# Feed-forward's tail in two halves, the projection's statistics one tile later, and the first experts' rows asked for a block ahead with their stores on ScalarE

## The chip, the cores and the metric

The kernel is one program on one core of a Trainium2 chip. The metric is device time in microseconds (us), the median of the runs. TensorE has two clock levels, 1.2 and 2.4 GHz; the profile gives the granted clock as a share of the higher one.

## The reference

A graph network over 3125 rows of 256 numbers and 53125 edges, four residual stages in a row:

```
x = x + gnn0(layernorm(x))     # attention over edges, projection, LN1, feed-forward, LN2
x = x + moe0(layernorm(x))     # 8 experts, top 2, hidden 256
x = x + gnn1(layernorm(x))     # two graph convolutions
x = x + moe1(layernorm(x))     # 8 experts, top 2, hidden 1024
```

The change lies in the end of gnn0 and in moe0:

```
h1  = layer_norm(h + attn_out, ln1_g, ln1_b)          # h is layernorm(x); attn_out = out @ Wp + bp
ffn = gelu(h1 @ W1 + b1) @ W2 + b2                    # 256 -> 1024 -> 256
x   = x + layer_norm(h1 + ffn, ln2_g, ln2_b)
t   = layernorm(x);  p = softmax(t @ router_w.T)
out = t + sum over the top 2 experts e of  w_e * (gelu(t @ w1[e] + b1[e]) @ w2[e] + b2[e])
x   = x + out
```

All of it is in float32.

## The kernel before

Rows are kept in SBUF in 25 tiles of 128 (`NT`), X (the residual), R (work) and ST (the statistics of `bn_stats`, six numbers a tile and partition). Each stage is a `Block` in which every engine has its own instruction list; a stage begins when all engines have left the one before. Within it, engines are ordered by semaphores alone (`wait_ge`, `then_inc`), and each engine takes its instructions strictly in order. SyncE (SP) issues nearly all plain DMAs, GpSimd (POOL) the indirect ones. `Chain` makes every step of VectorE (DVE) wait for the one before it.

**Projection, `attention_out` (L1094).** For each tile VectorE divides the sums by the weights (L1131, two tiles ahead), TensorE turns the tile and multiplies it by Wp (L1169, L1178), ScalarE (ACT) copies the turned tile in between (L1159), and VectorE adds h (L1140), adds the bias and writes R (L1144), then takes R's statistics (L1147). L1144 waits for L1140 and L1147 for L1144. `over_tiles` runs the first two tiles straight, then eleven loop rounds of two, then the last.

**Feed-forward, `ffn_blocks` (L1186).** 13 blocks of two tiles (`BR` = 2, the last holds one real tile). VectorE's step j: `prepare(j+1)` (normalise two tiles L612, times gamma L1240, plus beta L1243), copy of the turned block (L1249), then when TensorE has y(j): add the rows (L1257), add b2 and write R (L1260), statistics of R (L1264). TensorE's step j: eight hidden products (L1302), the turn of block j+1 (L1292), which needs `prepare(j+1)`, then y (L1311). ScalarE does the eight gelus (L1279). Before and after it `finish_ln` (L199) turns ST into RSTD and NMR with seven small steps of VectorE and a Sqrt of ScalarE.

**The tail, `ffn` (L1388).** In five chunks of 6, 6, 5, 5 and 3 tiles: ScalarE normalises R (L1419), VectorE multiplies by gamma (L1440), GpSimd adds beta to X (L1431), VectorE adds R to X (L1442) and takes X's statistics (L1445). `Logits` (L1320) follows tile by tile once a chunk's X is there: TensorE turns it (L1355), ScalarE copies it (L1381), TensorE multiplies it by the router (L1362). Before the first turn stands a product of ones with the router's weights (L1368). The router's weights are SyncE's second DMA of the block (L1342), after gamma and beta (L1408).

**First experts, `experts(k, 0)` (L1695).** GpSimd scatters the normalised rows to slots in HBM that are sorted by expert (L1826), and raises `landed` after each group of four tiles. Blocks of 256 slots are run in an order computed on the chip, 29 of them here (j = 0 to 28), each with a table word that gives its slot and its expert (`block_of`, a table load on the engine that asks). For block j:

- SyncE, `step`: `load_rows(j)` (waits for the turn of block j-2 and for `landed`; L1767), waits for y(j-2) by `y_done`, `store(j-2)` (waits for `y_ready`; L1778), `load_rest(j)` (L1772). All in this order, in one queue.
- ScalarE: waits for y(j-1), copies the weights of block j+1 from `every` to `pack` (L1915), then two gelus (L1926).
- TensorE: hidden product (L1958), turn of block j+1 (L1943, needs its rows), y (L1967). The turn writes the one buffer `pT`, which VectorE copies (L1860).
- VectorE: copy of the turned block (L1860), y plus b2 (L1870), which must find its y buffer stored.

GpSimd gathers the results back per group of tiles once the stores it needs have landed (L1846), and after the last block VectorE sums each tile's two results with the residual (L1877, L1883) and takes statistics (L1888). In the second experts layer (`layer` = 1) the same functions run with larger weights.

Of the kernel before, what the change touches and what calls it, by code (L numbers as in the profile page):

```python
# [189 lines left out]
def at(i, n=1):  # L190
    return bass.ds(i, n)
# [902 lines left out]
def attention_out(k):  # L1094
# [3 lines left out]
    with ExitStack() as s:  # L1098
# [87 lines left out]
def ffn_blocks(k):  # L1186
# [5 lines left out]
    nc, a, C, R, ST = k["nc"], k["a"], k["C"], k["R"], k["ST"]  # L1192
# [8 lines left out]
    BLOCKS = -(-NT // BR)  # L1201
    with ExitStack() as s:
# [19 lines left out]
        y_ready, fin, norm, scaled = sem("_y_ready"), sem("_finish"), sem("_norm"), sem("_scaled")  # L1222
        block = s.enter_context(nc.Block())

        @block.sync
        def _(sp):
            sp.dma_start(gb[:], a["rows0"][:, 1:3, :]).then_inc(gb_in, 16)
            sp.dma_start(pack[:], a["ffn"][0]).then_inc(pack_in, 16)

        @block.vector  # L1230
        def _(dve):
# [19 lines left out]
            def step(j, b, i, first, last):  # L1251
# [11 lines left out]
                for r in range(BR):  # L1263
                    dve.bn_stats(ST[:, at(BR * j + r), :], R[:, at(BR * j + r), :])  # L1264

            dve.wait_ge(gb_in, 16)
# [3 lines left out]
            over_tiles(dve, step, BLOCKS)  # L1270

        @block.scalar
        def _(act):
# [9 lines left out]
            over_tiles(act, step, BLOCKS)  # L1283
# [104 lines left out]
def ffn(k):  # L1388

    nc, a, X, R, ST = k["nc"], k["a"], k["X"], k["R"], k["ST"]  # L1390
    finish_ln(k, "1")
    ffn_blocks(k)
    finish_ln(k, "2")
    with ExitStack() as s:
        gb = s.enter_context(nc.sbuf_tensor("ln2_rows", [P, 2, D], F32))
        gb_in, normed = s.enter_context(nc.semaphore("ln2_rows_in")), s.enter_context(nc.semaphore("normed"))
        step_done, x_ready = s.enter_context(nc.semaphore("ffn_step")), s.enter_context(nc.semaphore("ffn_x_ready"))
        b_added = s.enter_context(nc.semaphore("ln2_b_added"))
        chunks_ = [(c, slice(lo, hi)) for c, (lo, hi) in enumerate(((0, 6), (6, 12), (12, 17), (17, 22), (22, NT)))]
# [3 lines left out]
        def wide(part):  # L1403
            return [P, part.stop - part.start, D]

        @block.sync
        def _(sp):
            sp.dma_start(gb[:], a["rows0"][:, 3:5, :]).then_inc(gb_in, 16)  # L1408
# [7 lines left out]
        def _(act):  # L1416
            for c, part in chunks_:
# [9 lines left out]
        @block.gpsimd  # L1427
        def _(pool):
            pool.wait_ge(gb_in, 16)
            for c, part in chunks_:  # L1430
                pool.tensor_tensor(X[:, part, :], X[:, part, :], gb[:, 1:2, :].to_broadcast(wide(part)),  # L1431
                                   ALU.add).then_inc(b_added, 1)

        @block.vector
        def _(dve):
            link = Chain(dve, step_done)
            dve.wait_ge(gb_in, 16)
            for c, part in chunks_:
                dve.wait_ge(normed, c + 1)
                link(dve.tensor_tensor(R[:, part, :], R[:, part, :], gb[:, 0:1, :].to_broadcast(wide(part)), ALU.mult))  # L1440
                dve.wait_ge(b_added, c + 1)
# [253 lines left out]
def experts(k, layer):  # L1695
# [17 lines left out]
    with ExitStack() as s:  # L1713
# [45 lines left out]
        def _(sp):  # L1759
# [19 lines left out]

            def step(j, b, i, first, last):  # L1780
# [19 lines left out]
            n = over_blocks(sp, step)  # L1800
            e = load_rows(2 * n + 1, 1, 2 * n)
            store(2 * n - 1, 1, 2 * n)
            load_rest(e, 1)
            store(2 * n, 0, 2 * n + 1)
            for landed_, count in [(y_out[0], n + 1), (y_out[1], n), (rows_in[0], n + 1), (rows_in[1], n + 1),
                                   (rest_in[0], n + 1), (rest_in[1], n + 1)]:
# [105 lines left out]
        def _(act):  # L1912
# [4 lines left out]
            def step(j, b, i, first, last):  # L1917
# [16 lines left out]
            over_blocks(act, step)  # L1934
# [578 lines left out]
```

## Time and profile before

| | |
|---|---|
| median of three runs | 2792.26 us (2792.14 to 2793.42) |
| the profiled execution | 2789.74 us, span 2787.7 us |
| TensorE (PE) busy | 2289.8 us, 82% of the span |
| VectorE (DVE) busy | 1490.0 us, 53% |
| ScalarE (ACT) busy | 1246.7 us, 45% |
| GpSimd (POOL) busy | 716.6 us, 26% |
| granted clock, mean | 0.927 |
| projection, start of the first division to the last statistics | 1053.3 to 1107.2 us |
| feed-forward's blocks, first hidden product to last statistics | 1120.0 to 1309.5 us |
| tail of the feed-forward, first DMA to copied logits | 1312.5 to 1361.7 us |
| first experts, first turn to the turn after the last block | 1409.1 to 1547.7 us |

The busy shares are means over stages with different limits and say little about any one of them. Times in the rows are microseconds from the start of the span. `PEld` is TensorE's weight load, which runs beside its products; `SPq` is an instruction of SyncE's queue. A pair in square brackets is the time that the engine was idle before the instruction and what released it.

### The profile page before, as it was taken

The page shows a single profiled execution, that of the slowest core. Times are in us where ns is not written, and L with a number is a line of the kernel's source. Part 1 is how long each engine was busy: PE and PEld are TensorE (multiplying, and loading weights), DVE is VectorE, ACT ScalarE, POOL GpSimd, SP SyncE. Part 2 cuts the span into 40 slices and gives each one's busy share as a digit, 9 for nine tenths or more (in the row PEclk, how much of TensorE's full clock was granted, in tenths as well). Part 3 has the DMA queues.
Part 4 walks back from the last instruction along what each step waited for, and adds up shares of the span by engine and source line. Part 5 has one row for each costly group of instructions (what it writes and reads, how often), then busy time and mean ns, then how long its engine had stood idle before and what let it go on. Part 6 is the DMA issues. An engine that isn't in the chain of part 4 may idle for free. (4 is left out here: it accounts for less than half of the span.)

```text
span 2787.7 us, 50123 instructions
## 1 busy us (share of the span) xinstructions
PE 2289.8 (82%) x10903; PEld 1803.5 (65%) x10904; DVE 1490.0 (53%) x2999; ACT 1246.7 (45%) x2511; POOL 716.6 (26%) x720
## 2 busy tenths in 40 slices
PE   1688876889989895997468399995999954999995
PEld 0344443666666663886456288884888853888884
DVE  7799975898888887332733644544002153111113
ACT  1799943777777772223223122343324431222221
POOL 0000011777777770000374311000110006002013
PEclk9999997999999998999589699997999956999998
DMA  5421222777777770000166322221222105656555
GB/s 196 200 76 73 76 82 81 208 212 213 212 212 212 213 203 20 22 0 4 49 212 193 109 76 70 69 67 53 67 67 74 55 2 189 218 191 221 189 204 178
DMA packets 183896, 353.28 MB, mean 127 GB/s; under 512 B 55346, under 2 KB 138727, under 8 KB 179111
## 3 DMA queue, kind: packets, MB, share of 16 engines
q1 hardware_dynamic: 138328, 206.94, 22.9%
q0 software_dynamic: 45520, 145.80, 18.1%
q8 instruction: 18, 0.29, 0.0%
q14 instruction: 30, 0.25, 0.0%
HBM read 275.32 MB, written 77.31 MB: 126 GB/s over the span
## 5 line engine op out<-in xcount | busy, mean ns | idle before, releaser
L2279 PE MATMUL gnn_p<-gnn_y,gnn_counts_wide 128*128 (+1 forms) x2500 | 553.6, 381 | 2.7 <-DVE R_kept L2161 2.6
L2279 PEld LDWEIGHTS gnn_p<-gnn_y,gnn_counts_wide 128*128 128x128 f32 x2500 | 473.1, 191 | 69.1 <-DVE R_kept L2161 6.6
L856 POOL DMA_INDIRECT kv_pair<-kv,gather_idx x448 | 428.1, 956 | 150.6 <-issue 103.6
L2084 ACT CAST gnn_counts_wide<-gnn_counts 128x1664 f32<-128x1664 uint16 x100 | 158.0, 1580 | 387.1 <-PE gnn_p L2279 368.0
L956 PE MATMUL p_edge_q<-QX_kept,onehot_turned 128*128 x904 | 264.1, 415 | 61.6 <-ACT onehot_turned L919 54.7
L1926 ACT ACTIVATE experts_hidden<-experts_p_hidden,experts_pack 128x256 f32<-128x256 f32 x290 | 134.1, 472 | 337.3 <-PE experts_p_hidden L1958 337.3
L1958 PE MATMUL experts_p_hidden<-experts_turned,experts_pack 128*128 128x256 f32 x1160 | 263.6, 383 | 2.1 <-DVE experts_turned L1857 1.2
L956 PEld LDWEIGHTS p_edge_q<-QX_kept,onehot_turned 128*128 128x128 f32 x904 | 155.4, 191 | 166.6 <-issue 151.1
L1967 PE MATMUL experts_p_y<-experts_pack,experts_hidden 128*128 128x256 f32 x1160 | 260.2, 379 | 0.0
L1958 PEld LDWEIGHTS experts_p_hidden<-experts_turned,experts_pack 128*128 128x128 f32 x1160 | 222.7, 192 | 33.6 <-issue 2.8
L964 PE MATMUL p_sums<-R_kept 128*128 128x264 f32 x896 | 237.3, 388 | 0.0
L564 PE MATMUL adj_p<-adj_onehot_src,adj_onehot_key 128*128 128x416 f16 x1200 | 231.4, 343 | 6.3 <-DVE adj_onehot_src L538 4.6
L1967 PEld LDWEIGHTS experts_p_y<-experts_pack,experts_hidden 128*128 128x128 f32 x1160 | 215.9, 190 | 27.3 <-ACT experts_hidden L1926 0.2
L1846 POOL DMA_INDIRECT experts_back<-slots_out,CSLOT x100 | 97.5, 975 | 417.0 <-issue 416.4
L908 ACT ACTIVATE dst_distance<-WHERE_kept,DST_kept 128x128 f32 x456 | 158.3, 394 | 67.2 <-issue 67.1
L538 DVE TENSOR_SCALAR adj_onehot_src<-adj_count_src,adj_src_in_quarter 128x832 f16<-128x832 f16 x500 | 181.3, 430 | 0.0
L1857 DVE TENSOR_SCALAR experts_turned<-experts_p_turned,experts_rest 128x256 f32<-128x256 f32 x60 | 29.8, 539 | 278.6 <-DMA experts_rest<-experts 252.4
L564 PEld LDWEIGHTS adj_p<-adj_onehot_src,adj_onehot_key 128*128 128x128 f16 x1200 | 110.0, 98 | 94.4 <-DVE adj_onehot_src L538 5.3
L883 DVE TENSOR_TENSOR qk_prod<-kv_pair,p_edge_q 128x528 f32<-128x528 f32 x224 | 156.2, 697 | 20.4 <-DMA kv_pair<-kv,gather_idx 14.1
L964 PEld LDWEIGHTS p_sums<-R_kept 128*128 128x128 f32 x896 | 153.4, 191 | 15.0 <-DVE ACC_kept L875 0.3
L888 DVE TENSOR_REDUCE qk_sum<-qk_prod 128x16 f32<-128x528 f32 x224 | 155.6, 694 | 0.0
L2253 POOL TENSOR_TENSOR R_kept<-gnn_y,gnn_brows 128x256 f32 x50 | 39.2, 784 | 451.8 <-DVE gnn_y L2137 438.1
(376 smaller groups left out, 3214.2 us busy)
## 6 DMA issues: line engine op xcount, KB each, us to landing
experts_pack<-experts SPq DMA_DIRECT2D x29, 2052.0 KB, 8.8
gnn_counts<-adj SPq DMA_DIRECT2D x400, 104.0 KB, 2.2
adj<-adj_counts SPq DMA_DIRECT2D x100, 208.0 KB, 1.9
experts_rows<-slots_in SPq DMA_DIRECT2D x60, 256.0 KB, 3.8
slots_out<-experts_y SPq DMA_DIRECT2D x58, 256.0 KB, 7.7
experts_rest<-experts SPq DMA_DIRECT2D x60, 130.0 KB, 8.0
kv_pair<-kv,gather_idx POOLq DMA_INDIRECT x448, 3.8
slots_in<-R_kept SPq DMA_DIRECT2D x2, 3328.0 KB, 13.9
```

What stands on the lines that cost most here:

```text
L538: ins = dve.tensor_scalar(ohs[p][:, c, :], count[:], column(smod, t + c), None, ALU.is_equal)
L564: mm = pe.matmul(pA[p][:, c, 0:QS // 2], ohk[p][:, n, :], ohs[p][:, n, c * (QS // 2):(c + 1) * (QS // 2)], start=False, stop=False)
L856: pool.indirect_dma_start(kv[r][:, j, :], None, a["kv"], bass.IndirectOffsetOnAxis(ap=idx[r][:, j:j + 1], axis=0)).then_inc(kv_in[r], 16)
L883: dve.tensor_tensor(prod[:], kv[r][:, :, 0:QW], pQ[q][:, :, 0:QW], ALU.mult).then_inc(prod_ready, 1)
L888: dve.tensor_reduce(red[q][:].rearrange("p j h -> p (j h)"), prod[:].rearrange("p j (h c) -> p (j h) c", c=HD + 1), AX.X, ALU.add).then_in ...
L908: ins = act.activation(dist[q][:, j, :], where[:, at(w), :].squeeze(1), ACT.Square, scale=-1.0, bias=column(k["DST"], t + j))
L956: mm = pe.matmul(pQ[q][:, j, 0:QW], oht[q][:, j, :], QX[:, at(w), :].squeeze(1), start=True, stop=True)
L964: mm = pe.matmul(pA[q][:, 0:VW], oh[r][:, j, :], wv[r % 4][:, j, :], start=(j == 0), stop=(j == GT - 1))
L1958: mm = pe.matmul(pH[c][:, 0:BT], w[:, lo:lo + P], tT[b][:, d, :], start=(d == 0), stop=(d == KD - 1))
L1967: mm = pe.matmul(pY[b][r][:, 0:D], hid[b][:, h, r * P:(r + 1) * P], w[:, W2 + h * D:W2 + (h + 1) * D], start=(h == 0), stop=(h == HC - 1))
L2084: act.copy(wide[b][:], raw[r][:].rearrange("p q s -> p (q s)")).then_inc(wide_ready, 1)
L2279: mm = pe.matmul(bank[:, off:off + D], wide[b][:, j * P:(j + 1) * P], y[:, at(n), :].squeeze(1), start=first and off == 0, stop=last and ( ...
```

## The change

Four edits.

1. *Projection.* `bn_stats` of tile n-1 is placed between L1140 and L1144 of tile n; that of the last tile follows the loop.
2. *Feed-forward.* Gamma and beta of the second LN are loaded at the start of `ffn_blocks`, and GpSimd adds beta to all of X there. After step 5 (of 0 to 12) VectorE works out the variance of tiles 0 to 11, ScalarE takes its root after its step 6, and VectorE finishes the factors after its own step 6. After each of the steps 7 to 12 VectorE finishes two of these tiles (`add_early`): normalise, times gamma, add to X, statistics of X.
3. *Tail.* Only tiles 12 to 24 are left to finish, in chunks of 5, 4 and 4. Tiles 0 to 11 need no wait before their turn. After normalising each chunk ScalarE copies four turned tiles of the first twelve, then the rest.
4. *First experts.* SyncE's `light_step(j)` asks for the rows of block j+1, waits for y(j-2) by `y_ready`, and asks for the rest of block j. The stores are issued by ScalarE: `store(j-1)` after the gelus of block j. The rows asked for past the last block stay, the rest asked for past it does not. The second experts layer keeps its order.

```diff
@@ attention_out, VectorE's step
+                if not first or b:
+                    spread_of(n - 1)
                 dve.wait_ge(part_ready, n + 1)
                 dve.scalar_tensor_tensor(out=R[:, at(n), :], ...).then_inc(r_ready, 1)
+
+            def spread_of(n):
                 dve.wait_ge(r_ready, n + 1)
                 dve.bn_stats(ST[:, at(n), :], R[:, at(n), :])
...
             over_tiles(dve, step)
+            spread_of(NT - 1)
@@ ffn_blocks
+    HALF = (BLOCKS - 1) // 2
+    EARLY = BR * HALF
...
             sp.dma_start(pack[:], a["ffn"][0]).then_inc(pack_in, 16)
+            sp.dma_start(ln2[:], a["rows0"][:, 3:5, :]).then_inc(ln2_in, 16)
+
+        @block.gpsimd
+        def _(pool):
+            pool.wait_ge(ln2_in, 16)
+            for lo in range(0, NT, 5):
+                pool.tensor_tensor(X[:, lo:lo + 5, :], X[:, lo:lo + 5, :], ln2[:, 1:2, :].to_broadcast([P, 5, D]),
+                                   ALU.add).then_inc(ln2_added, 1)
...
+            def add_early(p):
+                tiles = at(BR * p, BR)
+                for r in range(BR):
+                    tile = R[:, at(BR * p + r), :]
+                    normalise(dve, k, tile, tile, BR * p + r).then_inc(early_normed, 1)
+                dve.wait_ge(early_normed, BR * p + BR)
+                dve.tensor_tensor(R[:, tiles, :], R[:, tiles, :], ln2[:, 0:1, :].to_broadcast([P, BR, D]),
+                                  ALU.mult).then_inc(early_scaled, 1)
+                dve.wait_ge(early_scaled, p + 1)
+                dve.tensor_tensor(X[:, tiles, :], X[:, tiles, :], R[:, tiles, :], ALU.add).then_inc(early_x, 1)
+                dve.wait_ge(early_x, p + 1)
+                for r in range(BR):
+                    dve.bn_stats(ST[:, at(BR * p + r), :], X[:, at(BR * p + r), :])
...
-            over_tiles(dve, step, BLOCKS)
...
+            with dve.Fori(1, HALF // 2) as i:
+                step(2 * i, 0, i, False, False)
+                step(2 * i + 1, 1, i, False, False)
+            early_variance()
+            step(HALF, 0, HALF // 2, False, False)
+            early_factors()
+            dve.wait_ge(ln2_added, NT // 5)
+            with dve.Fori(HALF // 2, HALF - 1) as i:
+                step(2 * i + 1, 1, i, False, False)
+                add_early(2 * i - HALF)
+                step(2 * i + 2, 0, i + 1, False, False)
+                add_early(2 * i - HALF + 1)
+            step(BLOCKS - 2, 1, HALF - 1, False, False)
+            add_early(HALF - 2)
+            step(BLOCKS - 1, 0, HALF, False, True)
+            add_early(HALF - 1)
@@ ffn_blocks, ScalarE, after its step 6
+            act.wait_ge(var_ready, 1)
+            act.activation(small[:, 4, :], k["VAR"][:, 0:EARLY], ACT.Sqrt, bias=k["EPSC"][:, 0:1]).then_inc(std_ready, 1)
@@ ffn
+        early = 12
...
-        chunks_ = [(c, slice(lo, hi)) for c, (lo, hi) in enumerate(((0, 6), (6, 12), (12, 17), (17, 22), (22, NT)))]
+        chunks_ = [(c, slice(lo, hi)) for c, (lo, hi) in enumerate(((early, 17), (17, 21), (21, NT)))]
...
                 ins.then_inc(normed, 1)
-                if c:
-                    logits.scalar(act, chunks_[c - 1][1])
-            logits.scalar(act, chunks_[-1][1])
+                logits.scalar(act, slice(4 * c, 4 * c + 4))
+            for _, part in chunks_:
+                logits.scalar(act, part)
@@ experts, SyncE
+            def light_step(j, b, i, first, last):
+                load_rows(j + 1, 1 - b, j)
+                _, e = block_of(nc, mybir.EngineType.SP, k, j)
+                if not first:
+                    sp.wait_ge(y_ready, j - 1)
+                    sp.sem_inc(tally, 1)
+                load_rest(e, b)
...
+            else:
+                load_rows(0, 0, 0)
+                n = over_blocks(sp, light_step)
@@ experts, ScalarE
+                if not layer and not (isinstance(j, int) and j == 0):
+                    store(j - 1, 1 - b, j)
+
+            def store(j, b, ready):
+                slot, _ = block_of(nc, mybir.EngineType.Activation, k, j)
+                act.wait_ge(y_ready, ready)
+                act.dma_start(slots_out[at(slot)].squeeze(0), y[b][:]).then_inc(y_out[b], 16)
```

## Rows read from the trace of the kernel before

**Rows 1.** Windows of two stretches: busy us (instructions) by engine, granted clock, DMA share, GB/s.

```profile
1340.00:1361.70 21.70, 20.47 (x102) 19.72 (x101) 10.94 (x19) 9.90 (x26) 0.00 (x0) 0.50 0.00 0
...
1420.00:1450.00 30.00, 25.83 (x126) 20.93 (x125) 8.68 (x18) 10.72 (x18) 21.08 (x23) 1.00 0.75 236
```

**Rows 2.** Timeline of the projection: start, us, engine, line, operation [idle before, releaser].

```profile
1081.29 0.42 DVE L1131 TENSOR_TENSOR attn_rows<-ACC_kept,inv_weights 128x256 f32 x1 [0.18 <-issue]
...
1081.64 0.47 DVE L1140 SCALAR_TENSOR_TENSOR proj_part<-X_kept,RSTD_kept,p_proj 128x256 f32<-128x256 f32 x1
...
1082.25 0.48 DVE L1144 SCALAR_TENSOR_TENSOR R_kept<-proj_part,NMR_kept,proj_b 128x256 f32 x1
...
1082.88 0.43 DVE L1147 BATCH_NORM_STATS2 ST_kept<-R_kept  x1
...
1083.23 0.41 DVE L1131 TENSOR_TENSOR attn_rows<-ACC_kept,inv_weights 128x256 f32 x1
...
1083.96 1.04 PE L1178 MATMUL p_proj<-proj_w,attn_turned 128*128 128x256 f32 x4
...
1085.40 0.42 DVE L1131 TENSOR_TENSOR attn_rows<-ACC_kept,inv_weights 128x256 f32 x1 [0.18 <-issue]
```

**Rows 3.** Timeline of a feed-forward block, in its steady part.

```profile
1221.99 7.07 PE L1302 MATMUL ffn_p_hidden<-ffn_turned,ffn_weights 128*128 128x256 f32 x32
...
1236.24 7.07 PE L1302 MATMUL ffn_p_hidden<-ffn_turned,ffn_weights 128*128 128x256 f32 x32
...
1237.31 0.47 ACT L1279 ACTIVATE ffn_hidden<-ffn_p_hidden,ffn_weights 128x256 f32<-128x256 f32 x1 [7.73 <-PE ffn_p_hidden L1302]
...
1238.92 0.73 DVE L612 TENSOR_SCALAR ffn_rows<-R_kept,RSTD_kept,NMR_kept 128x256 f32 x2
...
1240.42 0.69 DVE L1243 TENSOR_TENSOR ffn_rows<-ffn_rows,ffn_affine_rows 128x512 f32<-128x512 f32 x1
...
1242.94 0.57 PEld L1292 LDWEIGHTS ffn_p_turned<-C_kept,ffn_rows 128*128 128x128 f32 x4
```

**Rows 4.** Timeline from the feed-forward's end through its tail.

```profile
1309.81 1.28 ACT L231 ACT_TABLE_LOAD   x1 [8.97 <-PEq L1202]
...
1315.34 1.02 PE L1368 MATMUL logits_p_raw<-logits_w,C_kept 128*128 128x8 f32 x4 [8.11 <-DMA logits_w<-router]
...
1319.37 18.83 POOL L1431 TENSOR_TENSOR X_kept<-X_kept,ln_rows 128x1536 f32<-128x1536 f32 x5 [279.09 <-issue]
...
1322.88 4.89 DVE L1442 TENSOR_TENSOR X_kept<-X_kept,R_kept 128x1536 f32<-128x1536 f32 x1 [5.45 <-POOL X_kept L1431]
...
1347.18 0.67 PE L1355 MATMUL logits_p_turned<-C_kept,X_kept 128*128 128x128 f32 x2
...
1359.13 0.67 PE L1355 MATMUL logits_p_turned<-C_kept,X_kept 128*128 128x128 f32 x2
```

**Rows 5.** Waits between 1414 and 1550: us in total, times, longest.

```profile
PE experts_p_turned L1943 <- DMA experts_rows<-slots_in: 18.1, 23, 1.8
```

**Rows 6.** Timeline of one block of the first experts.

```profile
1455.06 1.05 ACT L1915 COPY experts_pack<-experts_every 128x1026 f32 x1 [2.83 <-PE experts_p_y L1967]
...
1456.38 0.35 SPq L1772 DMA_DIRECT2D experts_rest<-experts  x1
...
1458.47 0.38 SPq L1767 DMA_DIRECT2D experts_rows<-slots_in  x1
...
1461.34 0.66 PE L1943 MATMUL experts_p_turned<-C_kept,experts_rows 128*128 128x128 f32 x4 [0.49 <-DMA experts_rows<-slots_in]
```

**Rows 7.** Timeline of TensorE's turns in the first experts.

```profile
1414.55 0.60 PE L1943 MATMUL experts_p_turned<-C_kept,experts_rows 128*128 128x128 f32 x4
...
1525.36 0.66 PE L1943 MATMUL experts_p_turned<-C_kept,experts_rows 128*128 128x128 f32 x4 [1.64 <-DMA experts_rows<-slots_in]
...
1529.41 0.66 PE L1943 MATMUL experts_p_turned<-C_kept,experts_rows 128*128 128x128 f32 x4
...
1547.72 0.66 PE L1943 MATMUL experts_p_turned<-C_kept,experts_rows 128*128 128x128 f32 x4
```

More of the change, by code:

```diff
@@ L1263, in step, with early_variance, early_factors @@
                 for r in range(BR):
-                    dve.bn_stats(ST[:, at(BR * j + r), :], R[:, at(BR * j + r), :])
+                    dve.bn_stats(ST[:, at(BR * j + r), :], R[:, at(BR * j + r), :]).then_inc(spread, 1)
+            def early_variance():
+                msum, diff, m2, sq = (small[:, c, :] for c in range(4))
+                st = ST[:, 0:EARLY, :]
+                dve.wait_ge(spread, EARLY)
+                link(dve.tensor_tensor(msum, st[:, :, 1], st[:, :, 4], ALU.add))
+                link(dve.tensor_tensor(diff, st[:, :, 1], st[:, :, 4], ALU.subtract))
+                link(dve.tensor_tensor(m2, st[:, :, 2], st[:, :, 5], ALU.add))
+                link(dve.tensor_tensor(sq, diff, diff, ALU.mult))
+                link(dve.tensor_scalar(m2, m2, 1.0 / D, None, ALU.mult))
+                dve.scalar_tensor_tensor(out=k["VAR"][:, 0:EARLY], in0=sq, scalar=0.25, in1=m2, op0=ALU.mult,
+                                         op1=ALU.add).then_inc(var_ready, 1)
+            def early_factors():
+                rstd = k["RSTD"][:, 0:EARLY]
+                dve.wait_ge(std_ready, 1)
+                link(dve.reciprocal(rstd, small[:, 4, :]))
+                link(dve.scalar_tensor_tensor(out=k["NMR"][:, 0:EARLY], in0=small[:, 0, :], scalar=-0.5, in1=rstd,
+                                              op0=ALU.mult, op1=ALU.mult))
+            def add_early(p):
[11 more added lines that the diff above has]
+                    dve.bn_stats(ST[:, at(BR * p + r), :], X[:, at(BR * p + r), :])
+            link = Chain(dve, small_step)
             dve.wait_ge(gb_in, 16)
@@ L1269, in _ @@
             dve.wait_ge(pack_in, 16)
[L1270 removed]
+            step(0, 0, 0, True, False)
+            step(1, 1, 0, True, False)
+            with dve.Fori(1, HALF // 2) as i:
[14 more added lines that the diff above has]
+            add_early(HALF - 1)
         @block.scalar
@@ L1282, in _ @@
             act.activation(y[0][:, 0, 0:1], k["EPSC"][:], ACT.Gelu)
-            over_tiles(act, step, BLOCKS)
+            step(0, 0, 0, True, False)
+            step(1, 1, 0, True, False)
+            with act.Fori(1, HALF // 2) as i:
+                step(2 * i, 0, i, False, False)
+                step(2 * i + 1, 1, i, False, False)
+            step(HALF, 0, HALF // 2, False, False)
+            act.wait_ge(var_ready, 1)
+            act.activation(small[:, 4, :], k["VAR"][:, 0:EARLY], ACT.Sqrt, bias=k["EPSC"][:, 0:1]).then_inc(std_ready, 1)
+            with act.Fori(HALF // 2, HALF - 1) as i:
+                step(2 * i + 1, 1, i, False, False)
+                step(2 * i + 2, 0, i + 1, False, False)
+            step(BLOCKS - 2, 1, HALF - 1, False, False)
+            step(BLOCKS - 1, 0, HALF, False, True)
         @block.tensor
@@ L1436, in _ @@
             link = Chain(dve, step_done)
-            dve.wait_ge(gb_in, 16)
             for c, part in chunks_:
                 dve.wait_ge(normed, c + 1)
-                link(dve.tensor_tensor(R[:, part, :], R[:, part, :], gb[:, 0:1, :].to_broadcast(wide(part)), ALU.mult))
-                dve.wait_ge(b_added, c + 1)
+                link(dve.tensor_tensor(R[:, part, :], R[:, part, :],
+                                       ln2[:, 0:1, :].to_broadcast([P, part.stop - part.start, D]), ALU.mult))
                 dve.tensor_tensor(X[:, part, :], X[:, part, :], R[:, part, :], ALU.add).then_inc(x_ready, 1)
@@ L1799, in _ @@
                 sp.dma_start(pack[0][:, 0:G], a[name][at(e), :, 0:G].squeeze(0)).then_inc(pack_in[0], 16)
[L1800 to L1804, printed above, removed]
+            if layer:
+                n = over_blocks(sp, step)
+                e = load_rows(2 * n + 1, 1, 2 * n)
+                store(2 * n - 1, 1, 2 * n)
+                load_rest(e, 1)
+                store(2 * n, 0, 2 * n + 1)
+            else:
+                load_rows(0, 0, 0)
+                n = over_blocks(sp, light_step)
             for landed_, count in [(y_out[0], n + 1), (y_out[1], n), (rows_in[0], n + 1), (rows_in[1], n + 1),
-                                   (rest_in[0], n + 1), (rest_in[1], n + 1)]:
+                                   (rest_in[0], n + 1), (rest_in[1], n + 1 if layer else n)]:
                 sp.wait_ge(landed_, 16 * count)
@@ L1933, in _ @@
                 copy_weights(0, 0)
-            over_blocks(act, step)
+            n = over_blocks(act, step)
+            if not layer:
+                store(2 * n, 0, 2 * n + 1)
         @block.tensor
```

28 lines of the change are left out of this document (11 added, 17 removed).

## The prediction, made before the changed kernel had run

> **What bounds the kernel now.** I read the windows by stage first, then the timeline inside each stage that the diff touches, then the waits of the first experts layer. Elsewhere the program is the same, so the sum is over four stretches, each on the path by itself because a block's end waits for all engines. *First experts*: 30 us of them have the DMA engines busy to 0.75, TensorE to 25.83 [rows 1]; neither is full. *Projection*: the timeline of VectorE [rows 2] shows one tile: rows of the tile after next (L1131), partial sum (L1140), R (L1144), statistics (L1147). Between starts lie 0.35, 0.61, 0.63 and 0.35 us. The two long ones are steps that wait for the result just before them; an independent step starts about 0.08 before its predecessor has ended (bn_stats starts at 1082.88, lasts 0.43, the next step starts at 1083.23). VectorE's chain of dependent steps bounds it: two tiles take 1085.40 - 1081.29 = 4.11 us. *Feed-forward*: TensorE's runs follow without idle, 1236.24 - 1221.99 = 14.25 us a block; what VectorE must finish in time is `prepare`, which ends at 1240.42 + 0.69 = 1241.11 while TensorE's turn starts at 1242.94 [rows 3]: 1.83 us of slack. *Its tail*: TensorE has its router product of ones at 1315.34 but cannot turn tiles before 1327.8, when X of the first chunk is there after GpSimd's and VectorE's adding; from there it is the loop of turn, ScalarE's copy and router product, ten tiles in 1359.13 - 1347.18 = 11.95 us [rows 4]. *The experts' turns*: TensorE waits for rows at 23 of them, 18.1 us in all [rows 5]. In [rows 6] rows are asked for 2.09 us after the rest's DMA (SyncE's table loads and checks lie between), which itself stands behind the wait for the y of two blocks back; they are used 2.87 us later, at a turn that stood idle for them. The wait is due to the place in the queue.
>
> **The change part by part.**
>
> *Projection.* `bn_stats` of tile n-1 goes between L1140 and L1144, so neither it nor L1144 waits for the instruction before it. New distances: 0.35 (L1131 to L1140), 0.40 (0.48 less the overlap of 0.08), 0.35, 0.40, together 1.50, and the loop's return, which is the difference of the two halves of the pair now (2.17 against 1.94: 0.23). A pair is 3.23 instead of 4.11, 0.88 less; 11 pairs in the loop give 9.7, the first tiles 0.3: **-10.0 us**. What is late next is TensorE: the projection released by the L1131 at 1083.23 ends at 1083.96 + 1.04 = 1085.00, 1.77 later, and in the new order L1140 asks for it 1.50 + 0.35 = 1.85 after. It fits by 0.08, so I take the full gain, but each 0.1 us more in that round trip costs 2.4: ends -5 and -11.
>
> *Feed-forward, second half.* `add_early` stands after steps 7 to 12: two normalisations, one wide multiplication, one wide addition, two bn_stats. The first three shapes take 1241.11 - 1238.92 = 2.19 us in `prepare` [rows 3]; two bn_stats 0.35 + 0.43; three waits with address arithmetic some 0.1 each (estimate from the 0.15 between L1144's end and L1147 [rows 2]), little more: 3.2 us. After steps 7 to 10 a `prepare` stands behind it on VectorE, and TensorE's turn behind that: 3.2 - 1.83 = 1.4 us of stall, four times: **+5.6**. After step 11 nothing waits (a block's time until the next y). After step 12 it stands alone on the path: **+3.2**. With a stall of 0.8 or 2.0 the four are 3.2 or 8.
> `early_variance` is six short steps before step 6. No VectorE step of these rows is nearer to its follower than 0.35, so six are at most 2.1 against 1.83 of slack: 0, at most 0.3. The Sqrt on ScalarE with a table load before and one after it, 1.28 each [rows 4], stands where ScalarE idles 7.73 [rows 3]: 0, at most 1.3 in each of two loop rounds if the load is placed ahead of a gelu.
> GpSimd's additions (five, 18.83 us [rows 4]) move from the tail to the first two blocks. Their rows come as third DMA of SyncE's queue, behind the weights for which TensorE waits anyway; nobody else is behind them. 18.8 us are 1.3 blocks, so they may overlap VectorE's work on the first y, where a turn waits with 1.83 of slack. VectorE's X addition of the tail that met GpSimd took 4.89 us [rows 4]; here three short steps have two SBUF inputs. I take 0, since most of the additions fall where VectorE idles; ends 0 and +5.
> The Trainium skill (SBUF — State Buffer, Who interferes with whom) says that a VectorE instruction with two SBUF inputs and a GpSimd instruction that reads SBUF exclude each other for the whole of one. The 4.89 us agree with it. By this rule each of the three steps could wait one GpSimd step out.
>
> *The tail by halves.* X of tiles 0 to 11 and the bias are ready at the block's start, so the first turn follows the router's weights and the product of ones: 1315.34 + 1.02 = 1316.4. 24 tiles at 1.195 are 28.7 (one stop for three tiles' normalising is in that pace); two more for four tiles cost some 0.7 each (estimate, a third of normalising them), 1.4. Last turn at 1346.5 against 1359.13 [rows 4]: **-12.6**. VectorE's parts (5, 4 and 4 tiles) are ready well before their turns, with GpSimd gone. Ends -11 and -15. TensorE's clock was granted 0.50 here, its 1.2 GHz level, although it was busy 20.47 of 21.7 us [rows 1]; I take the same level.
>
> *First experts.* rows(j+1) go ahead of SyncE's wait for y and of the rest; the store leaves SyncE, and the wait for y's end with it. SyncE's round becomes some 1.3 (rows to rest) and 2.09 (rest to rows), 3.4 us, under TensorE's round. Rows are then asked for more than a period before their turn instead of 2.87 us, the wait goes, and TensorE is next. Where the turn did not wait, a block took 1529.41 - 1525.36 = 4.05. From turn 1 at 1414.55 to turn 29 at 1547.72 are 133.2 us [rows 7]; 28 x 4.05 = 113.4: **-19.8**, which agrees with the 18.1 of waits. What follows (gathers, sums) starts from the last block's y and shifts with it. The store on ScalarE: behind both gelus of block j it loads the table, waits for y(j-1), added on VectorE by then, and issues. Behind it on ScalarE stands the weight copy of the next round, for which TensorE waits. ScalarE idled 2.83 before that copy at a period of 4.6 [rows 6], so 2.3 at 4.05, less some 0.5 between y's end and the copy: room for 1.8. No DMA is issued by ScalarE in this trace; the nearest rows are SyncE's, 0.35 and 0.38 an issue [rows 6], and with table load and arithmetic I take 1.1: it fits, by 0.7. Ends: -22 (period 3.97) and -9 (4.44).
> The Trainium skill (DMA: Bandwidth & Descriptors, Issuing engines are not separate DMA queues) says that DMAs started by several engines run on the same 16 DMA engines and only the sequencer's time is saved. It would speak against this change if the rows' transfer were the limit. No run here shows that yet; it is a rival below.
>
> **Sum.** -10.0 + 5.6 + 3.2 - 12.6 - 19.8 = -33.6. The profiled execution took 2789.74 us (span 2787.7), so it would take 2756.1; the median of the runs shown, 2792.26, is 2.5 above it, and for that I predict **2758.7 us**.
>
> **Rivals.**
> *Transfers bound the experts.* Rows asked for earlier land later, because scatter, gather, stores and rests share the engines. For: the engines' 0.75 at some 4.7 us a block [rows 1] scales to 0.87 at 4.05, and the longest wait is 1.8 [rows 5]. Against: that leaves some room, and rows gain a period of time. Period 4.4: +10, so 2768; none of the gain: 2778.
> *The projection's round trip binds*, half its gain is lost: 2763.7. For: 0.08 us of margin.
> *GpSimd's additions stall block 1, or the stalls are longer.* +5: 2764.
> *TensorE's clock rises in the tail,* as the work is denser, and the pace falls below 1.195; each 0.1 is 2.4 us: about 2752.
> *ScalarE becomes the bound (the other side).* If the store takes s on ScalarE, its round is 0.5 + 1.8 + s against 4.05; it decides from s = 1.8. The other parts give -13.8, so the kernel is slower than before from a period of 4.76 + 13.8 / 28 = 5.25, s = 3.0, and by over 0.2% from s = 3.2: some 2798 us. Against: the same DMA costs SyncE 0.4. At s = 2.3 the time is 2774.
> *The change doesn't do what it says* (rows still behind something): 2778; the diff leaves only the turn two blocks back and the scatter ahead of them.
>
> **How the numbers follow.** As summed, sizes off by a few us (2750 to 2766): 0.62. Projection's or GpSimd's rival: 0.13. Transfers: 0.12. Clock or larger gains, under 2750: 0.07. ScalarE somewhat late: 0.03; so late that the kernel is slower: 0.02; nothing gained: 0.01. The range 2747 to 2773 leaves out most of the last cases and the worst of the transfers. About 0.2%, 5.6 us, is what a measurement of this kernel tells from no change. Faster by more: 0.96; within: 0.02; slower: 0.02.
>
> **What would show it.** Two projection tiles in 3.2 us; the turns of blocks 9 to 12 of the feed-forward late by 1.4 behind `prepare`, and no others; the first turn for the logits some 4 us after its block's start; no wait for rows at the experts' turns and 4.05 between them; ScalarE's issue well before y's end. The prediction is wrong if the experts' turns still wait, if ScalarE's copy starts later than 0.6 after y, or if the projection's pair stays over 3.6.

## The result, and the profile after

| | before | after |
|---|---|---|
| median of three runs | 2792.26 us | 2753.51 us (2753.1 to 2756.55) |
| span of the profiled execution | 2787.7 us | 2751.3 us |
| mean granted clock | 0.927 | 0.928 |

The ratio is 0.9865, with a 95% interval of 0.9841 to 0.9888: faster by 38.75 us. Forecast were 33.6 us and 2758.7, range 2747 to 2773.

The stretches are read as before. The projection, in the timeline (start, us, engine, line, operation):

```profile
1059.52 0.42 DVE L1131 TENSOR_TENSOR attn_rows<-ACC_kept,inv_weights 128x256 f32 x1
1059.90 0.48 DVE L1140 SCALAR_TENSOR_TENSOR proj_part<-X_kept,RSTD_kept,p_proj 128x256 f32<-128x256 f32 x1
1060.29 0.42 DVE L1151 BATCH_NORM_STATS2 ST_kept<-R_kept  x1
1060.63 0.47 DVE L1146 SCALAR_TENSOR_TENSOR R_kept<-proj_part,NMR_kept,proj_b 128x256 f32 x1
1061.01 0.42 DVE L1131 TENSOR_TENSOR attn_rows<-ACC_kept,inv_weights 128x256 f32 x1
...
1062.73 0.43 DVE L1131 TENSOR_TENSOR attn_rows<-ACC_kept,inv_weights 128x256 f32 x1
```

A pair of tiles takes 1062.73 - 1059.52 = 3.21 us where [rows 2] had 4.11: the gaps of 0.61 and 0.63 are gone. From first division to last statistics the stage is 42.8 us, before 53.8.

The feed-forward's start, where GpSimd now adds, and block 9 with the added steps:

```profile
1106.38 15.19 POOL L1246 TENSOR_TENSOR X_kept<-X_kept,ln_rows 128x1280 f32<-128x1280 f32 x5 [69.19 <-DMA ln_rows<-rows]
...
1106.47 3.34 DVE L1259 TENSOR_TENSOR ffn_rows<-ffn_rows,ffn_affine_rows 128x512 f32<-128x512 f32 x1
1109.84 3.27 DVE L1262 TENSOR_TENSOR ffn_rows<-ffn_rows,ffn_affine_rows 128x512 f32<-128x512 f32 x1
...
1223.90 0.72 DVE L612 TENSOR_SCALAR R_kept<-R_kept,RSTD_kept,NMR_kept  x2
...
1226.97 0.72 DVE L612 TENSOR_SCALAR ffn_rows<-R_kept,RSTD_kept,NMR_kept 128x256 f32 x2
...
1229.20 0.66 PE L1374 MATMUL ffn_p_turned<-C_kept,ffn_rows 128*128 128x128 f32 x4 [0.87 <-DVE ffn_rows L1262]
```

One early addition takes 1226.97 - 1223.90 = 3.07 us, and the turn behind it came late, with an idle of 0.87 and a block of 15.35 instead of the 14.25 of [rows 3]. From the first hidden product to the last y the stage grew from 187.2 to 190.8 us.

The tail:

```profile
1298.72 0.72 DVE L612 TENSOR_SCALAR R_kept<-R_kept,RSTD_kept,NMR_kept 128x256 f32<-128x256 f32 x2
...
1306.19 1.02 PE L1450 MATMUL logits_p_raw<-logits_w,C_kept 128*128 128x8 f32 x4 [9.69 <-DMA logits_w<-router]
1307.06 1.09 PE L1437 MATMUL logits_p_turned<-C_kept,X_kept 128*128 128x128 f32 x4
...
1336.31 0.67 PE L1437 MATMUL logits_p_turned<-C_kept,X_kept 128*128 128x128 f32 x2
```

The first turn follows the product of ones at once. From the end of the last early addition (1301.67) to the last turn are 34.6 us; before it was 49.6 from the last statistics (1309.53) to 1359.13 [rows 4].

One block of the first experts, and its windows (busy us by engine, granted clock, DMA share, GB/s) beside those of the tail:

```profile
1431.70 1.05 ACT L1997 COPY experts_pack<-experts_every 128x1026 f32 x1 [2.24 <-PE experts_p_y L2058]
...
1432.66 0.83 ACT L2008 ACTIVATE experts_hidden<-experts_p_hidden,experts_pack 128x256 f32<-128x256 f32 x2
1432.70 0.60 PE L2034 MATMUL experts_p_turned<-C_kept,experts_rows 128*128 128x128 f32 x4
...
1433.50 0.38 ACTq L2016 DMA_DIRECT2D slots_out<-experts_y  x1
1434.21 0.37 SPq L1837 DMA_DIRECT2D experts_rows<-slots_in  x1
...
1436.73 0.60 PE L2034 MATMUL experts_p_turned<-C_kept,experts_rows 128*128 128x128 f32 x4
```

```profile
1316.50:1338.50 22.00, 21.64 (x109) 21.14 (x108) 4.60 (x9) 8.30 (x22) 0.00 (x0) 0.50 0.00 0
1400.00:1430.00 30.00, 29.61 (x147) 25.01 (x146) 10.74 (x22) 12.87 (x22) 21.59 (x21) 1.00 0.80 251
```

Turns lie 4.03 us apart here, and no turn waits for rows any more. TensorE is busy 29.61 of 30 us (before 25.83 [rows 1]), the DMA engines 0.80. From turn 1 to turn 29 are 114.5 us, before 133.2 [rows 7].

### The profile page after: what moved, and what is told of

It reads as the page before. It is cut to its first block and busy times, and to the rows that moved or that the text cites. A ratio compares the mean times of both kernels' runs of the same rounds, so it can differ in the third digit from the quotient of the medians.

```text
span 2751.3 us, 50173 instructions
## 1 busy us (share of the span) xinstructions
PE 2287.4 (83%) x10903; PEld 1804.4 (66%) x10904; DVE 1492.0 (54%) x3027; ACT 1242.6 (45%) x2503; POOL 710.1 (26%) x720
## 5 line engine op out<-in xcount | busy, mean ns | idle before, releaser
L2049 PEld LDWEIGHTS experts_p_hidden<-experts_turned,experts_pack 128*128 128x128 f32 x1160 | 222.8, 192 | 33.6 <-issue 2.8
```

The costliest lines, as they stand in the source:

```text
L2049: mm = pe.matmul(pH[c][:, 0:BT], w[:, lo:lo + P], tT[b][:, d, :], start=(d == 0), stop=(d == KD - 1))
```

## The experiments

The runs fell on four chips. On two of them the kernel before took 2792.47 and 2789.77 us, as in the result; on the other two (called the slower chips below) it took 3164.51 and 3130.44 us. What differs there is shown with the first experiment. Totals are compared only with the kernel before on the same chip; besides them I compare stretches in the traces, since on the first of the slower chips the runs of one kernel spread over 16 to 23 us.

### One part of the change at a time

Each is the kernel before with one part of the diff: the projection's hunks, those of `ffn_blocks` and `ffn`, or those of `experts`.

- only_projection: `spread_of(n - 1)` between L1140 and L1144.
- only_ffn: `early_variance`, `early_factors`, `add_early`, GpSimd's additions in `ffn_blocks`, the tail in chunks 12-17-21-25.
- only_experts: `light_step`, `load_rows(0, 0, 0)`, `store()` on ScalarE.

> The kernel before with the projection's edit alone. Theory: a pair of tiles takes 3.23 us instead of 4.11 and the time falls by the 10.9 us by which the stage got shorter in the two traces, give or take 1, so about 2781.5 us. Rival (the gain is given back by the wait on the first feed-forward tiles or by the gathers behind): under 8 us.

> The kernel before with the feed-forward's edit alone (first half's statistics and additions inside the loop, tail for the second half). Theory, by the two traces: +3.5 us inside the loop, +3.1 for the last add_early, and the tail's turns 15.0 shorter from the last statistics on, so -8.5 us in all, time about 2784. Rival (the stall at the turns came from the profiler or from transfers of the other edits): loop +0, time about 2780.

> The kernel before with the experts' edit alone (rows a block ahead, stores issued by ScalarE). Theory: blocks of 4.09 us instead of 4.76, -18.7 us, time about 2773.5. The three parts alone then give -10.9, -8.5 and -18.7, -38.1 in all, against -38.75 of the whole change. Rival (the parts lean on each other, or one of them also moves a stage that it does not touch, such as the gathers or the sum of experts): their sum misses the whole by over 3 us.

Measured on one chip, before 3164.51 us (3153.68 to 3176.99):

| | median | ratio, 95% | projection, first product to last statistics | first hidden product to last turn of logits | first experts, first to last turn |
|---|---|---|---|---|---|
| only_projection | 3158.58 | 0.9968 (0.9952 to 0.9984) | 40.7 | 239.0 | 195.7 |
| only_ffn | 3157.71 | 0.9966 (0.9948 to 0.9985) | 51.1 | 231.8 | 194.4 |
| only_experts | 3160.06 | 0.9976 (0.9960 to 0.9993) | 51.7 | 239.7 | 189.7 |
| before, in the result | | | 51.7 | 239.4 | 139.0 |
| after, in the result | | | 40.7 | 230.9 | 120.4 |

Projection and feed-forward each move their own stretch, by 11.0 us (expected 10.9) and 7.6 (expected 8.5) against the kernel before of the result, and neither moves the two other stretches of the table by over 2 us. The experts' part missed: 5 to 6 us in its stretch instead of 18.7. The medians of the whole fell by 5.9, 6.8 and 4.5 us, 17.2 together; the whole change wasn't run on this chip, so whether the parts add up to it stays open here. The experts' stretch is longer on this chip with every kernel, by 55 to 57 us in the old order and by 69 in the new. Where it got longer is seen at VectorE's additions of y and at GpSimd, in only_experts:

```profile
1734.85 0.76 DVE L1882 TENSOR_TENSOR experts_y<-experts_p_y,experts_rest 128x256 f32<-128x256 f32 x2 [1.25 <-PE experts_p_y L1988]
...
1742.90 0.76 DVE L1882 TENSOR_TENSOR experts_y<-experts_p_y,experts_rest 128x256 f32<-128x256 f32 x2 [1.24 <-PE experts_p_y L1988]
...
1750.98 0.76 DVE L1882 TENSOR_TENSOR experts_y<-experts_p_y,experts_rest 128x256 f32<-128x256 f32 x2 [1.24 <-PE experts_p_y L1988]
...
1756.37 1.00 POOL L1858 DMA_INDIRECT experts_back<-slots_out,CSLOT  x1 [29.90 <-issue]
```

From 1726 to 1756 GpSimd issues no indirect DMA, and two blocks take 8.05 and 8.08 us, 4.03 each. Once its gathers run, four blocks took 24.8, 24.9 and 24.0 us in only_experts, and 23.7, 25.9 and 25.8 with the blocks of before (only_ffn): the order of requests hardly matters any more. From turn to turn, three of the four blocks of only_experts still take 3.9 to 4.6 us, and one takes 12 to 13. This is what stands in such a one (timeline):

```profile
1785.15 0.60 PE L1964 MATMUL experts_p_turned<-C_kept,experts_rows 128*128 128x128 f32 x4
...
1792.51 0.47 ACT L1938 ACTIVATE experts_hidden<-experts_p_hidden,experts_pack 128x256 f32<-128x256 f32 x1 [4.51 <-remote]
1792.71 0.69 DVE L1872 COPY experts_turned<-experts_p_turned 128x512 f32<-128x512 f32 x1 [8.16 <-remote]
```

The turn ended at 1785.75, the hidden products at 1785.31, and VectorE's copy, which waits for these alone, began 7 us later; ScalarE's second gelu is late in the same way. `remote` means that the view finds no instruction behind the release. This isn't a wait for rows: from 1750 to 1870 us no turn of only_experts waits for rows, while in only_ffn turns waited 19.5 us for them from 1740 to 1870. The new order took these waits away, and the time went into idle time of several engines at once instead. The attention's gathers show longer idle times too, in the page's groups, first only_experts, then the changed kernel on a chip like that of the result:

```profile
L856 POOL DMA_INDIRECT kv_pair<-kv,gather_idx x448 | 430.4, 961 | 399.5 <-DVE R_kept L866 249.3
```

```profile
L856 POOL DMA_INDIRECT kv_pair<-kv,gather_idx x448 | 426.1, 951 | 150.4 <-issue 101.1
```

GpSimd's issues last as long; it idles 399.5 us before them instead of 150.4. The rival that late rows bound the experts is thus wrong for the new order on this chip as well. What stops the engines beside gathers there, and whether slow transfers are behind it, was not found out.

### The changed kernel once more

> The changed kernel itself, on the chip of these runs, where the gathers of the attention and of the experts took far longer than in the two profiles of the result. Theory: projection and feed-forward gain what they gained there (11 and 8.4 us), the experts only in the blocks that lie beside no GpSimd transfer (0.55 us each in some 9 to 10 blocks, about 5 us, as the part alone showed: 189.7 against 194.4 us), so about 24 us less than before. Rival (the experts' gain is whole here too, and the part alone was disturbed): 36 to 39 us less.

These runs fell on a chip like that of the result, so the condition of the theory wasn't met: 2754.09 us (2752.54 to 2755.56) against 2792.47, ratio 0.9857 (0.9833 to 0.9881), 38.4 us less. First to last turn of the experts: 120.7 us. The gain of the experts' part is whole there, as the rival had it for the chip at hand; it says nothing of the slower ones.

### What bounds the experts' block: the request ahead, or the store's move

```diff
@@ stores_moved_only, from after: light_step
-                load_rows(j + 1, 1 - b, j)
-                _, e = block_of(nc, mybir.EngineType.SP, k, j)
+                e = load_rows(j, b, j - 1)
...
@@ rows_ahead_only, from after: light_step; ScalarE's store() goes
-                    sp.wait_ge(y_ready, j - 1)
-                    sp.sem_inc(tally, 1)
+                    store(j - 2, b, j - 1)
...
```

> The changed kernel, but SyncE asks for a block's rows in that block's own turn, as before, while ScalarE issues the stores. Theory: the rows were late because SyncE reached their request only after the store's wait for y; with the store gone from its queue most of the experts' gain stays, and the blocks take 4.1 to 4.3 us (the changed kernel's 4.09, before 4.76). Rival (it is the request a block ahead that hides the landing of the rows, 3.8 us in the profile before): the blocks stay at 4.5 us or more.

> The changed kernel, but SyncE issues the stores again, with the rows still asked for a block ahead. Theory: the rows are then early whatever SyncE waits for, and only SyncE's own work in a block (four issues and their address work, about 4.2 us) can set the pace: 4.1 to 4.3 us for a block. Rival (the store's wait on SyncE is what holds the rows, even a block ahead): 4.5 us or more.

One run each, on the chip where before took 3130.44 us; they took 3122.25 and 3120.2. In the seven blocks without gathers the additions of y lie 4.23 us apart on average with the stores moved alone (3.99 to 4.51), and 4.02 with the rows ahead alone; before it was 4.56 (only_ffn), changed 4.03. Waits in those blocks, stores_moved_only:

```profile
PEld experts_p_turned L2033 <- DMA experts_rows<-slots_in: 2.6, 5, 0.8
PE experts_p_turned L2033 <- DMA experts_rows<-slots_in: 0.6, 2, 0.4
```

With the rows ahead alone there is no such line. Both rivals fall (4.5 us or more). The first theory holds, and the second came out a little better than its 4.1 to 4.3. In these blocks the stores' move alone gave 0.33 us of the gain of 0.53, the rows ahead alone all of it. But that needs a caution: with the rows ahead alone SyncE's own rounds, from one request for rows to the next, took 4.13 to 4.39 us, more than the blocks' 4.02. The lead of the requests covers that for eight blocks. Over 28 blocks it would hardly do (an estimate: 0.2 us a block makes 5 us, more than the one period by which rows are early). Whether the half that was left out matters over more blocks, or beside gathers, these two couldn't tell.

### The two moves that the trace after suggested

In the trace after, VectorE idles 5 us and more in each feed-forward block ahead of y, while the early additions stand in front of `prepare`; and ScalarE's weight copy stands in front of the gelus.

```diff
@@ early_between, from after: VectorE's step; the calls behind the steps go
                     copy_turned(j + 1, 1 - b)
+                if early is not None:
+                    add_early(early)
                 dve.wait_ge(y_done, j + 1)
...
@@ gelus_first, from after: ScalarE's step
-                else:
-                    wait_if(act, y_done, j)
-                    copy_weights(j + 1, 1 - b)
...
+                if not layer:
+                    wait_if(act, y_done, j)
+                    copy_weights(j + 1, 1 - b)
```

> The changed kernel, with each early addition moved inside the block, between the copy of the turned tiles and the wait for y, where VectorE was idle 5 us a block. Theory: the four stalls at the turns of blocks 9 to 12 go (0.74 to 0.89 each and 1.1 of block length, -4.3 us) and the last addition leaves the tail (-3.1): the stretch from the first hidden product to the first turn of the logits is 7 us shorter. Rival (the adds there delay y's own handling, and a stall comes back at the hidden products or at the y bank): 2 us shorter or less.

> The changed kernel with ScalarE's two gelus of block j ahead of its copy of the weights of block j+1 in the first experts. Theory: the y products wait no more for the gelus behind a late copy, and the blocks fall from 4.09 to the products' own 3.9 us, 4 to 5 us in all. Rival (the copy, begun later, is then the last thing before the next hidden product, or frees its source later): 4.09 or longer.

One run each, on the chip with 3130.44 us: 3113.46 and 3121.77 us. early_between: first hidden product to last turn 224.6 us, against 231.4 of stores_moved_only with the same feed-forward: 6.8 less, and no turn waits for VectorE. gelus_first: in the blocks without gathers the additions of y lie 3.89 us apart, not 4.03. Then both together, on the chip with 2792.47:

> The changed kernel with both of the moves tried singly: the early additions between the copy of the turned tiles and the wait for y, and ScalarE's gelus ahead of its weight copy. Theory: 6.8 us less from the first hidden product to the last turn of the logits, and 0.14 us less in each undisturbed experts' block (some 1.5 to 4 us), so 8 to 11 us less than the changed kernel on the same chip. Rival (the stages behind wait for something else and give it back): under 4 us less.

2744.22 us, ratio to before 0.9817 (0.9793 to 0.9841), 9.9 us less than the changed kernel on the same chip: the version that beats both. (Two of its runs, the profiled one among them, took 18 us longer, all of it ahead of the projection; the stretches below start later.) First hidden product to last turn: 224.9 against 231.6 of the changed kernel; experts' turns 115.6 against 120.7. A block of it:

```profile
1453.34 0.47 ACT L2003 ACTIVATE experts_hidden<-experts_p_hidden,experts_pack 128x256 f32<-128x256 f32 x1 [0.39 <-PE experts_p_hidden L2047]
1453.58 1.89 PE L2056 MATMUL experts_p_y<-experts_pack,experts_hidden 128*128 128x256 f32 x8
...
1453.87 1.05 ACT L1995 COPY experts_pack<-experts_every 128x1026 f32 x1
...
1457.47 1.89 PE L2056 MATMUL experts_p_y<-experts_pack,experts_hidden 128*128 128x256 f32 x8
```

The gelu ends (1453.81) before its copy starts (1453.87), and the y products lie 1457.47 - 1453.58 = 3.89 apart, TensorE's own pace.

### Stores on SyncE under the faster block

The two moves, with `store()` back on SyncE as in rows_ahead_only.

> The same two moves, with the first experts' stores issued by SyncE again and the rows still asked for a block ahead. It asks whether the stores' move to ScalarE is worth anything once the rows are early. Theory: SyncE's own round is 3.9 to 4.0 us, about the 3.89 us of the blocks, so the undisturbed blocks take 3.9 to 4.0 and the whole is within 2 us of the version with stores on ScalarE. Rival (SyncE's round is longer than the 4.02 us at which it ran unnoticed, or the store's wait delays the rows again): 4.1 or more, over 3 us longer.

2750.67 us, ratio 0.9845 (0.9821 to 0.9869): 6.4 us above the version with ScalarE's stores. The theory fell, the rival holds. Five of the first six blocks take 3.86 to 3.92 us (one 4.09), the later ones mostly 4.2 to 5.2. SyncE's requests and a turn (timeline), and the waits from 1415 to 1500 us:

```profile
1438.96 0.38 SPq L1835 DMA_DIRECT2D experts_rows<-slots_in  x1
...
1440.43 0.40 SPq L1846 DMA_DIRECT2D slots_out<-experts_y  x1
1441.07 0.35 SPq L1840 DMA_DIRECT2D experts_rest<-experts  x1
...
1443.29 0.37 SPq L1835 DMA_DIRECT2D experts_rows<-slots_in  x1
...
1446.91 0.66 PE L2024 MATMUL experts_p_turned<-C_kept,experts_rows 128*128 128x128 f32 x4 [1.06 <-DMA experts_rows<-slots_in]
...
1448.01 0.38 SPq L1835 DMA_DIRECT2D experts_rows<-slots_in  x1
```

```profile
PEld experts_p_turned L2024 <- DMA experts_rows<-slots_in: 12.9, 16, 2.0
DVE experts_y L1951 <- DMA experts_rest<-experts: 7.6, 6, 1.6
```

SyncE's own queue shows no wait at all in this stretch, and its round is 4.33 and 4.72 us here, and at least 4.13 between 1394 and 1504 us: with three issues and their table loads it is the bound. The lead of the first blocks is used up, then rows and rests come late. That is what the store's move to ScalarE is worth under blocks of 3.89 us, 6.4 us by the medians and 10.6 from first to last turn in the two traces; rows_ahead_only was too short of undisturbed blocks to show it.

### Room on ScalarE

```diff
                     store(j - 1, 1 - b, j)
+                if not layer:
+                    for m in range(2):
+                        act.copy(spare[b][m][:], every[:, m, :])
```

> The changed kernel with two idle copies of 1.05 us each added on ScalarE behind the store, into buffers that nothing reads, in every block of the first experts. Theory: between the store's issue and the next weight copy ScalarE has 1.3 to 1.6 us to spare, so two copies overrun it by 0.5 to 0.8 us and the undisturbed blocks take 4.5 to 4.9 us instead of 4.03. Rival (the room is 2.2 us, all of the idle time shown ahead of the copy): 4.03 to 4.1. Rival of the prediction's other side (ScalarE is already the bound of the changed block): 6.1.

2754.6 us, ratio 0.9858 (0.9821 to 0.9896) to the 2789.77 of its chip, no loss beside the changed kernel. Undisturbed blocks take 4.07 to 4.08 us:

```profile
1442.43 0.83 ACT L2009 ACTIVATE experts_hidden<-experts_p_hidden,experts_pack 128x256 f32<-128x256 f32 x2
...
1443.26 0.38 ACTq L2020 DMA_DIRECT2D slots_out<-experts_y  x1
1443.68 2.00 ACT L2015 COPY experts_spare<-experts_every 128x1026 f32<-128x1026 f32 x2 [0.43 <-issue]
...
1445.59 1.04 ACT L1998 COPY experts_pack<-experts_every 128x1026 f32 x1
```

My theory of 1.3 to 1.6 us of room fell, the rival of 2.2 holds: the store occupies ScalarE from 1443.26 to 1443.68, 0.42 us in all, and 2.0 us of copies fit behind it with a loss of 0.04 a block.

### GpSimd's additions laid over VectorE's steps

```diff
             pool.wait_ge(ln2_in, 16)
+            pool.wait_ge(y_done, 1)
```

> The changed kernel, but GpSimd's five additions into X begin only when y of block 0 is done, so that they lie beside the first blocks' steps and not beside the start of the stage. Theory A (GpSimd and VectorE exclude each other on their shared path to SBUF for a whole instruction): VectorE's wide steps of the next prepare take 3.3 us each instead of 0.7, twice or more, with a room of about 1.8 us in a block of 14.25; one block's turn waits 3 to 7 us and the time is 3 to 7 above the changed kernel's. Theory B (they only share bandwidth, and a step is slowed by a fraction): within 1.5 us of the changed kernel.

The whole took 3157.79 us on the first of the slower chips, where the changed kernel wasn't run, so the expectation is judged by the stretch. First hidden product to last y: 202.2 us against 191.3 of only_ffn on the same chip, 10.9 more. Timeline, and the longest wait:

```profile
1385.54 15.26 POOL L1247 TENSOR_TENSOR X_kept<-X_kept,ln_rows 128x1280 f32<-128x1280 f32 x5 [98.45 <-PE ffn_p_y L1394]
...
1386.20 2.79 DVE L1280 TENSOR_TENSOR R_kept<-ffn_y,ffn_weights 128x512 f32<-128x512 f32 x1
1389.02 0.75 DVE L1284 BATCH_NORM_STATS2 ST_kept<-R_kept 128x6 f32<-128x256 f32 x2
1389.69 5.09 DVE L612 TENSOR_SCALAR ffn_rows<-R_kept,RSTD_kept,NMR_kept 128x256 f32<-128x256 f32 x2
1394.82 3.25 DVE L1260 TENSOR_TENSOR ffn_rows<-ffn_rows,ffn_affine_rows 128x512 f32<-128x512 f32 x1
1398.10 3.25 DVE L1263 TENSOR_TENSOR ffn_rows<-ffn_rows,ffn_affine_rows 128x512 f32<-128x512 f32 x1
```

```profile
PE ffn_p_turned L1375 <- DVE ffn_rows L1263: 19.9, 2, 10.7
```

Theory A holds in kind and is surpassed in size: steps that take 0.69, 0.72 (the pair of L612), 0.69 and 0.69 elsewhere took 2.79, 5.09, 3.25 and 3.25, where one GpSimd addition takes 15.26 / 5 = 3.05, and a turn waited 10.7 us. The bn_stats between kept their 0.75. The 3 to 7 us counted only two such steps.

## Why the prediction was right

**Projection, -10.0.** Measured 11.0 on a stage of 53.8, shown by the part alone. The pair came to 3.21 us above and 3.19 further on, forecast 3.23; the rest of what I had too low was the straight tiles at both ends. TensorE's round trip, with 0.08 of margin, cost none of the forecast gain: VectorE idles 0.09 us once a pair ahead of its partial sum.

**Feed-forward, +5.6 and +3.2.** The mechanism came as forecast, at four turns and no others. The slack of 1.83 was read rightly and the addition took 3.07, forecast 3.2; the lengthening was 1.1 a block, not 1.4. The stretch grew by 3.5 us: four times 1.1, less 0.7 by which its first run of hidden products was shorter, agree within 0.2. The last addition cost 2.9 (last y to the end of the addition 5.2 us, before 2.3 to the last statistics). early_between, which takes both away, gained 6.8.

**GpSimd's additions, 0.** Right, but not for my reason. I let them begin behind the weights' DMA and reach over the first y. They began at 1106.38 and ended at 1121.57, just before that y, and stretched two steps of VectorE to 3.34 and 3.27 under TensorE's first products. pool_late shows what my upper end of +5 should have been: 11, had they begun 15 us later. The Trainium skill (SBUF — State Buffer, Who interferes with whom) has a VectorE instruction with two SBUF inputs and a GpSimd instruction that reads SBUF exclude each other for a whole instruction; these traces agree, with the durations above. The cover was luck of timing, and I had priced its loss too low.

**The tail, -12.6.** Measured -15.0. The first turn came 5.4 us after its block's last VectorE step, where I had 6.9, since the router's weights are now the first DMA of their block; and the pace was 1.17 us a tile, not 1.195, with two stops of 0.7 as forecast. The clock stayed at 0.50, the 1.2 GHz level, in the window above: the rival of a rising clock fell. The 21.64 us of 22 that TensorE was busy there changed nothing in it.

**First experts, -19.8.** Measured -18.7: 4.09 us a block instead of 4.05. The missing 0.04 a block belongs to blocks of 4.2 to 4.4 in which a y product waits for the gelus behind the weight copy, in the waits of the trace after:

```profile
PEld experts_p_y L2058 <- ACT experts_hidden L2008: 2.3, 6, 0.5
```

In six blocks of this trace the copy starts 0.77 to 0.93 us after the y product's end, in the others 0.46 to 0.59. A copy later than 0.6 was one of my signs of being wrong; it came true there and cost these blocks 0.2 to 0.3 us each. What held the copy back isn't shown. gelus_first takes the waits away. The reason given was right, that the rows' place in the queue made them late. That the transfers had room (0.75, now 0.80) was right on this chip. On the two slower ones the blocks beside gathers gained nothing, for a cause that I hadn't thought of and that stays open. The Trainium skill (DMA: Bandwidth & Descriptors, Issuing engines are not separate DMA queues) grants only the sequencer's time to an issue moved to another engine. The traces agree: it is SyncE's round, 4.1 us and more with three issues, that the move relieves. How much of the 18.7 belongs to the request ahead and how much to the store's move wasn't measured on this chip.

**The store on ScalarE, s = 1.1 with room for 1.8.** s is 0.42: no table load shows between the gelu's end and the issue, so that work seems to have been done while ScalarE's gelus ran. The room is at least 2.0. The other side of the forecast, s of 3.0, was far off.

**Sum.** -11.0 + 3.5 + 2.9 - 15.0 - 18.7 = -38.3, against -38.75 and, repeated, -38.4 of the medians. The profiled spans differ by 36.4 only: stages that the diff doesn't touch differed by a few us between the two executions (3.1 less ahead of the projection, 5.0 more in all behind the last of the experts' turns; in the repeat 3.0 less and 2.8 more). Why they did isn't shown. The tail's term was the one most mis-sized, by 2.4, in my favour and inside its end of -15.

## What to carry to other kernels

Ask first which queue a late transfer stands in, and what stands ahead of it: here moving one request ahead of the wait for y, and the store out of its queue, gave 18.7 us, and once rows were early and blocks faster still, the next bound was the issuing engine's own round (4.1 us and more with the stores back in it). Put added work into the stretch where its engine idles anyway, not behind the step that frees the next stage: the same additions took 6.8 us more behind the step than ahead of the wait for y. Two engines' additions on the same memory should be laid side by side only where neither is about to be waited for.

## What the runs showed of the hardware that I had not expected

- On two of four chips the same kernel took 12 to 13% longer. Nearly all of the difference lay in stages with GpSimd's indirect DMAs; the graph convolutions, which have none, took 644.5 us from their first product to the last and, in only_experts, 645.2. only_experts moved 145 GB/s at a share of 0.55 from 800 to 1000 us, the kernel before 212 GB/s at 0.79. In the experts' blocks VectorE stood idle over 8 us at a time there, with its inputs ready for 7. The cause stays open.
- A VectorE step of 0.69 us met by GpSimd's additions took 2.79 to 3.34 us, `TENSOR_SCALAR` with one tile as input too; bn_stats did not.
- A DMA issue takes 0.38 us on ScalarE and the next instruction starts 0.04 later, while SyncE needed 4.1 us and more for a round of three issues without a single wait.
